# Attention score masks: added by VectorE in the instructions that take the row maxima, instead of by TensorE matmuls

## What is computed

```
def sdpa(q, k, v, bias):                       # 16 heads of 16 features
    s = jnp.einsum('bhqd,bhkd->bhqk', q, k) * scale + bias
    p = jax.nn.softmax(s, axis=-1)
    return jnp.einsum('bhqk,bhkd->bhqd', p, v)

causal_bias = jnp.where(i[None, :] <= i[:, None], 0.0, NEG)       # self, 256 keys
allowed = (j <= seg_ids) & (j > seg_ids - LOOKBACK)               # cross, 4096 keys
cross_bias = jnp.where(allowed, 0.0, NEG)
for l in range(4):
    h = rmsnorm(x, n1[l]);  q, k, v = split(h @ Wqkv[l].T + bqkv[l]);  q, k = rope(q), rope(k)
    x = x + sdpa(q, k, v, causal_bias) @ Wo[l].T + bo[l]
    h2 = rmsnorm(x, n2[l])
    x = x + sdpa(h2 @ Wq_c[l].T, kc, vc, cross_bias) @ Wo_c[l].T  # kc, vc from memory @ Wkv_c[l].T
    h3 = rmsnorm(x, n3[l])
    x = x + silu(h3 @ Wg[l].T) * (h3 @ Wu[l].T) @ Wd[l].T
```

## Time and profile before

| | us |
|---|---|
| median of 3 runs | 621.46 (620.04 to 621.73) |
| span of the profiled execution, first to last instruction | 617.9 |
| TensorE busy | 564.1 (91%) |
| VectorE busy | 353.5 (57%) |
| ScalarE busy | 279.5 (45%) |
| GpSimd busy | 117.7 (19%) |
| mean granted TensorE clock | 0.991 of full |

### The profile page before, as it was taken

One profiled execution on the slowest core, in us unless ns is written; L12 is line 12 of the kernel. 1 busy time (PEld: TensorE's weight loads), 2 busy tenths in 40 slices (PEclk: granted clock), 3 DMA queues, 4 the chain that ended last, 5 costly groups with the idle time before them and its releaser, 6 DMA issues.

```text
span 617.9 us, 13676 instructions
## 1 busy us (share of the span) xinstructions
PE 564.1 (91%) x5806; PEld 421.8 (68%) x5806; DVE 353.5 (57%) x680; ACT 279.5 (45%) x490; POOL 117.7 (19%) x124
## 2 busy tenths in 40 slices
PE   4989998999999899999998989999898989999855
PEld 1666655988767566988766658987666558897523
DVE  5896445466564454674554455574554364752787
ACT  0254444633355336433544446342554547445523
POOL 4252100012323100020612000122312001252110
PEclk9999999999999999999999999999999999999969
DMA  8800020010500200201400200204000200000001
GB/s 334 345 2 25 12 69 2 5 65 1 205 2 4 102 1 3 68 1 27 180 1 36 70 2 2 69 1 189 16 2 1 71 0 2 0 1 2 2 1 39
DMA packets 4676, 30.29 MB, mean 49 GB/s; under 512 B 1153, under 2 KB 1665, under 8 KB 2818
## 3 DMA queue, kind: packets, MB, share of 16 engines
q1 hardware_dynamic: 4610, 29.35, 12.5%
HBM read 28.82 MB, written 0.52 MB: 47 GB/s over the span
## 4 chain that ended last, share of the span: by engine, by line
PE 77%; DVE 10%; ACT 8%; issue 3%; POOL 1%; DMA 1%; SPq 0%; DVEq 0%; POOLq 0%
PE psD L326 18%; PE QD L621 12%; PE psD L634 9%; PE QD L408 6%; PE QD L443 4%; ACT PTR L1253 3%; PE psD L320 3%; PE QD L436 3%; PE QD L394 3%; DVE AQ L1803 3%; PE psD L463 2%; PE QD L431 2%; PE psD L359 2%; PE psD L484 2%; PE psD L470 2%
## 5 line engine op out<-in xcount | busy, mean ns | idle before, releaser
L1253 ACT ACTIVATE PTR<-QD 128x2048 f32<-128x2048 f32 x40 | 75.1, 1878 | 41.8 <-PE QD L443 21.5
L326 PE MATMUL psD<-WAB,hT 128*128 128x256 f32 (+1 forms) x216 | 70.1, 465 | 2.2 <-DVE hT L1744 2.2
L2492 POOL TENSOR_TENSOR rstd<-ms,mhalf 128x2 f32<-128x2 f32 x26 | 19.9, 764 | 271.8 <-DVE ms L1729 270.6
L1803 DVE TENSOR_REDUCE AQ<-QD 128x8 f32<-128x2048 f32 (+1 forms) x24 | 55.0, 2290 | 27.0 <-PE QD L408 27.0
L621 PE MATMUL QD<-HH,WFH 128*128 128x256 f32 x224 | 67.4, 301 | 0.4 <-DVE WFL L1903 0.4
L1903 DVE TENSOR_TENSOR WFL<-WC,WFH 128x512 fp32r<-128x512 f32 x64 | 48.0, 755 | 32.2 <-ACT WFH L1297 32.1
L621 PE MATMUL QD<-HL,WFH 128*128 128x256 f32 x224 | 63.3, 283 | 0.0
L621 PE MATMUL QD<-HH,WFL 128*128 128x256 f32 x224 | 63.3, 283 | 0.0
L1800 DVE TENSOR_REDUCE AQ<-QD 128x16 f32<-128x2048 f32 x16 | 36.7, 2293 | 39.9 <-PE QD L408 39.9
L634 PE MATMUL psD<-WC,HID 128*128 128x256 f32 x256 | 58.2, 380 | 0.0
L326 PEld LDWEIGHTS psD<-WAB,hT 128*128 128x128 f32 x216 | 39.7, 195 | 21.0 <-issue 14.2
(11 more groups left out here) (172 smaller groups left out, 1021.2 us busy)
## 6 DMA issues: line engine op xcount, KB each, us to landing
WC<-in_wc SPq DMA_DIRECT2D x4, 3072.0 KB, 10.9
WAB<-in_wa SPq DMA_DIRECT2D x4, 1024.0 KB, 4.9
WAB<-in_wb SPq DMA_DIRECT2D x4, 1024.0 KB, 4.7
WF<-in_wf SPq DMA_DIRECT2D x1, 3072.0 KB, 22.8
bias<-in_bias SPq DMA_DIRECT2D x4, 512.0 KB, 3.4
WAB<-in_wt SPq DMA_DIRECT2D x1, 1024.0 KB, 6.0
X<-in_x SPq DMA_DIRECT2D x2, 256.0 KB, 2.8
out_x<-X SPq DMA_DIRECT2D x4, 128.0 KB, 2.4
```

The source lines that it names most:

```text
L326: mm = pe.matmul(bank(l, use)[:, col:col + n], lhs(k), rhs(k), start=(k == 0), stop=(k == KT - 1))
L1253: nc.scalar.activation(PTR[:, r % 2, :], QD[:, :], ACT.Exp, scale=SCALE).then_inc(t_exp, 1)
L1803: v = dve.tensor_reduce(QKR[b][:, t, 0, h, MAXROW].rearrange("p (s r) -> p r s", r=SG_H), QD[:, :].rearrange("p (r s n) -> p r s n", r=4, ...
```

## The change

The mask matmuls of `scores` go: the first score matmul of a bank now has `start=True`. `maxima` becomes a run of `tensor_tensor_reduce` instructions, one for each head and tile of queries. Each reads its 128 or 256 scores from PSUM, adds the mask (bf16, SBUF), multiplies by -1, writes the product back to the same place of PSUM, and keeps the running minimum; a second instruction then writes this minimum out. In the lists below the two are `ISA QD,AQ<-QD,causB` and `ISA AQ 128x1`. A round with tiles of 128 keys has 16 of the pairs, a round with 256 keys 8. `causB` grows to 128 x 256, zeros in its first half. The mask matmuls of `scores_T` (L431) stay.

```
@@ scores @@
                 quad_free(s_max, l * ROUNDS + r + 1)
-                for a in range(4):
-                    if cross:
-                        pe.matmul(quad[a].rearrange("p (s n) -> p s n", s=2), identB[:, :],
-                                  maskB[:, 2 * b:2 * b + 2, :].rearrange("p t n -> p (t n)").unsqueeze(1).broadcast_to([P, 2, L]),
-                                  start=True, stop=False, skip_group_check=True)
-                    elif t == 0:
-                        pe.matmul(quad[a].rearrange("p (s n) -> p s n", s=4), identB[:, :],
-                                  causB[:, :].unsqueeze(1).broadcast_to([P, 4, P]), start=True, stop=False, skip_group_check=True)
-                    else:
-                        pe.matmul(quad[a].rearrange("p (s n) -> p s n", s=2)[:, :, P:L], identB[:, :],
-                                  causB[:, :].unsqueeze(1).broadcast_to([P, 2, P]), start=True, stop=False, skip_group_check=True)
...
-                                           QKT[b][rows(a), s, L:L + keys], start=False, stop=True, skip_group_check=True)
+                                           QKT[b][rows(a), s, L:L + keys], start=(at == 0), stop=True, skip_group_check=True)
@@ maxima @@
                 if cross:
-                    v = dve.tensor_reduce(QKR[b][:, :, 0, h, MAXROW].rearrange("p t (s r) -> p r s t", r=SG_H),
-                                          QD[:, :].rearrange("p (r s t n) -> p r s t n", r=4, s=2, t=QT), AX_X, ALU.max, negate=True)
+                    if l == 0:
+                        dve.wait_ge(mask_set, 1)
+                    for a in range(4):
+                        for n, s in enumerate(ss):
+                            for q in range(QT):
+                                v = dve.tensor_tensor_reduce(quad[a][:, (2 * n + q) * P:(2 * n + q + 1) * P],
+                                                             quad[a][:, (2 * n + q) * P:(2 * n + q + 1) * P], maskB[:, 2 * b + q, :],
+                                                             -1.0, NO_MAX, ALU.add, ALU.min,
+                                                             accum_out=QKR[b][:, q, 0, SG_H * s + a, MAXROW:MAXROW + 1])
                 else:
...
+                    keys = (t + 1) * P
+                    for a in range(4):
+                        for n, s in enumerate(ss):
+                            v = dve.tensor_tensor_reduce(quad[a][:, n * keys:(n + 1) * keys], quad[a][:, n * keys:(n + 1) * keys], causB[:, L - keys:L],
+                                                         -1.0, NO_MAX, ALU.add, ALU.min,
+                                                         accum_out=QKR[b][:, t, 0, SG_H * s + a, MAXROW:MAXROW + 1])
@@ DVE, layer @@
                 residual(l, 0, "wo0")
-                cross_kv(l, 0)
+                maxima(l, 5)
                 mean_square(l, 1, 0)
-                maxima(l, 5)
```

More of the change, by code:

```diff
@@ L786, in layer @@
                 pv(l, 5)
+                cross_qT(l, 0, 1)
                 outputs_T(l, 5)
@@ L798, in layer @@
                 cross_kT(l, 1)
+                cross_qT(l, 1, 0)
                 pv(l, 6)
-                cross_qT(l, 1, 0)
+                scores(l, 8)
+                cross_qT(l, 1, 1)
                 outputs_T(l, 6)
-                scores(l, 8)
                 pv(l, 7)
-                cross_qT(l, 1, 1)
                 outputs_T(l, 7)
@@ L932, in _ @@
             cross_qT(0, 0, 0)
+            cross_qT(0, 0, 1)
             outputs_T(0, 4)
-            cross_qT(0, 0, 1)
             scores(0, 6)
             pv(0, 5)
+            outputs_T(0, 5)
             cross_kv(0, 1)
-            outputs_T(0, 5)
             scores(0, 7)
@@ L984, in rest @@
                 out_proj(0, 1, "cwo1", Woc, "coT1")
+                down(0, 0, range(0, 4))
                 gate_up(0, 0, 7)
-                down(0, 0, range(0, 4))
                 norm_T(0, 2, 1)
@@ L1043, in rest @@
                 maxima_T(NL - 1, 4)
-                cross_kT(NL - 1, 0)
                 pv(NL - 1, 3)
                 scores_T(NL - 1, 4)
+                outputs_T(NL - 1, 3)
+                maxima_T(NL - 1, 5)
                 norm_T(NL - 1, 1, 0)
-                maxima_T(NL - 1, 5)
-                outputs_T(NL - 1, 3)
+                cross_kT(NL - 1, 0)
+                scores_T(NL - 1, 5)
                 cross_q(NL - 1, 0)
-                scores_T(NL - 1, 5)
                 pv(NL - 1, 4)
                 cross_qT(NL - 1, 0, 0)
+                scores(NL - 1, 6)
                 cross_qT(NL - 1, 0, 1)
-                scores(NL - 1, 6)
                 outputs_T(NL - 1, 4)
@@ L1111, in rest @@
                 gate_up(NL - 1, 1, 4)
+                down(NL - 1, 1, range(0, 4))
                 gate_up(NL - 1, 1, 5)
@@ L1114, in rest @@
                 gate_up(NL - 1, 1, 7)
-                down(NL - 1, 1, range(0, 4))
                 window_T(0)
@@ L1374, in layer @@
                 self_strips(l, 1, 0, 1)
+                split_high(l, 0)
+                split_high(l, 1)
                 strip_outputs(l, 1)
@@ L2139, in layer @@
                 tokens_low(l, 0)
+                split_low(l, 2)
                 split_low(l, 3)
+                hidden(l, 0, 0)
                 split_low(l, 4)
-                hidden(l, 0, 0)
                 hidden(l, 0, 1)
                 split_low(l, 5)
+                divide(l, 8)
                 hidden(l, 0, 2)
-                divide(l, 8)
+                hidden(l, 0, 3)
                 divide(l, 9)
                 split_low(l, 6)
-                hidden(l, 0, 3)
                 hidden(l, 0, 4)
@@ L2153, in layer @@
                     all_blocks(l, 1)
+                residual(l, 1, "cwo1")
+                split_low(l, 8)
+                mean_square(l, 2, 1)
                 hidden(l, 0, 5)
-                residual(l, 1, "cwo1")
-                mean_square(l, 2, 1)
-                split_low(l, 8)
                 normalise(l, 2, 1)
@@ L2241, in rest @@
             def rest(further):
+                divide(0, 3)
                 weigh_T(0, 1, 0)
-                divide(0, 3)
+                split_low(0, 0)
                 cross_q(0, 0)
+                split_low(0, 1)
+                maxima(0, 6)
                 divide(0, 4)
-                maxima(0, 6)
                 divide(0, 5)
-                cross_kv(0, 1)
                 maxima(0, 7)
                 residual(0, 1, "wo1")
-                split_low(0, 0)
+                cross_kv(0, 1)
                 mean_square(0, 1, 1)
@@ L2255, in rest @@
                 cross_q(0, 1)
-                split_low(0, 1)
+                maxima(0, 8)
                 divide(0, 6)
-                maxima(0, 8)
                 divide(0, 7)
@@ L2378, in rest @@
                 hidden(NL - 1, 0, 0)
+                split_low(NL - 1, 5)
                 hidden(NL - 1, 0, 1)
-                split_low(NL - 1, 5)
-                hidden(NL - 1, 0, 2)
                 divide(NL - 1, 8)
@@ L2384, in rest @@
                 split_low(NL - 1, 6)
+                hidden(NL - 1, 0, 2)
                 hidden(NL - 1, 0, 3)
@@ L2651, in rest @@
                 causal(1, 0)
+                sines(1, 1, 0)
+                sines(1, 1, 1)
+                causal(1, 1)
+                causal(1, 2)
                 add_bo(1, 0)
-                sines(1, 1, 0)
-                causal(1, 1)
-                sines(1, 1, 1)
-                causal(1, 2)
                 causal(1, 3)
```

425 lines of the change are left out of this document (210 added, 215 removed).

## The result

| | before | changed |
|---|---|---|
| median, us | 620.75 (4 runs, 619.56 to 621.73) | 636.35 (4 runs, 634.92 to 638.09) |
| span of the profiled execution, us | 617.9 | 632.8 |
| TensorE / VectorE busy, us | 564.1 / 353.5 | 545.2 / 410.0 |
| mean granted TensorE clock | 0.991 | 0.973 |

The ratio is 1.0252, 95% interval 1.0234 to 1.027: slower.

A forecast was written before the change was run, and what follows sets the result against it. TensorE, busy 564.1 of 617.9 us, was taken as the bound, with maxima narrowly hidden in the QD loop. Adding 24.4 us gave 642.3, and 3.6 around it 646 us; the range was 610 to 682.

The forecast's parts named there:

- A pair of 0.27: VectorE's maxima: main instruction over 128 numbers 0.20 us, accumulator read-out 0.07 us more; 0.40 with 256 numbers.
- Both rivals: VectorE's pairs: read-out hidden, 0.20 to 0.23 us, chance 0.19; or PSUM both ways costs more, 0.30 to 0.34, chance 0.16.
- the slope of the prediction: 520 pairs taken to lie on the path, so each 0.01 us of a pair changes the time by 5.2 us.
- The sum: Whole kernel: +5.0 us a layer, 20 in four, +4.4 in the first layer; 617.9 + 24.4 = 642.3, plus 3.6 around it.
- waits in rounds 0 to 5: TensorE's new waits for longer maxima and lost cover in the first six attention rounds: 6.3 us a layer.
- The estimate of 0.32: Price of a VectorE pair by the skill's overhead figures, in us; it would make the sum some 26 us higher.
- Masks: Four mask matmuls leave each round's scores on TensorE: 7.8 us a layer, 31.3 us in four layers.
- Along the layer: TensorE's new order laid out stretch by stretch with the old lengths: +5.0 us a layer, 20 in four.
- the two signs of being wrong: Pairs under 0.22 us apart, or the waits of rounds 0 to 5 missing.
- the rival of cover in the new order: Rounds 0 to 5: the order hides the forecast waits, 6.3 us a layer, giving 621 us; chance 0.09.
- First layer: Rounds 0 to 3 there: longer maxima of 6.2 us wholly on the path, less 1.8 of waits: +4.4 us.
- The clock: Rival: TensorE's granted clock falls because it has more holes, giving 660 us or more; chance 0.03.

The follow-up runs named there:

- e9: The changed kernel with the product of each pair written to a bf16 tile in SBUF instead of back to PSUM: 613.26 us.
- e12: The old lists of steps with masks added in the pairs and the product in SBUF, f32 for the first bank's pairs in self rounds: 621.71 us.
- e2: The new lists of steps with TensorE's mask matmuls and the one reduction per round of the kernel before: 632.29 us.
- e3: The new lists of steps, no mask matmuls in scores, one reduction per round over unmasked scores: 600.98 us.
- e1: The old lists of steps, with masks added by VectorE in pairs and no mask matmuls in scores: 640.54 us.
- e10: The changed kernel with the old order of steps in the quantised part alone: 634.67 us.
- e6: The changed kernel with useless transposes filling TensorE's waits for the maxima in rounds 3, 5 and 7: 632.54 us.
- e4: The old lists of steps, no mask matmuls in scores, one reduction per round over unmasked scores: 592.49 us.
- e11: Old lists, no mask matmuls in scores, one reduction over unmasked scores, plus useless transposes in two TensorE waits of the quantised part: 593.35 us.
- e5: The changed kernel with one VectorE copy of 128x1 numbers between SBUF tiles ahead of each of the 512 pairs: 648.98 us.

## Why the prediction was right, point by point

**The forecast held; its price was off in two parts that nearly cancel.** A pair of 0.27 was 0.20 + 0.07. Measured is 0.25, which e9 and e12 split into 0.20 + 0.01 + 0.04. I took the read-out for seven times what it costs, by ScalarE's rows, and the write to PSUM for nothing. Both rivals were half true: the read-out is hidden, and the product in PSUM costs more, if only directly behind a read-out. Each alone would have given a pair of 0.21 or of 0.31. That the two nearly cancel is luck. By the slope of the prediction, 0.25 makes 646 - 10.4 = 635.6; 636.35 was measured. Put at 0.21, the same formula gives 646 - 31.2 = 614.8 for e9, which took 613.3. That it comes so close is partly luck too. The sum had nothing for the last stretch (4.5 us longer), for the stretch without rounds (1.1 a layer) and for the clock (3.8), and against that it had waits in rounds 0 to 5 that aren't there.

**Launch and end.** The sum adds 3.6 us for what lies around the span. That was a median less the span of another execution. In one and the same execution it is 1.7 to 1.9 us for the kernel before (beside the experiments), and 2.5 to 3.1 for the changed one, so about 1 us of the loss lies outside the span; what makes it longer isn't shown.

The estimate of 0.32 from the figures of the Trainium skill (Perfetto Trace Analysis, Optimizing Scalar/DVE Operations) is too high by 0.07 here. The second instruction is there in the trace, as the Trainium skill says of accumulator outputs (VectorE: DVE Perf Modes, Two Vector instructions with no wait between them), but lies almost wholly beside its neighbours.

**Masks.** 31.3 us by the sum, 31.3 by e2 and e3, 27.7 in the old lists.

**Along the layer.** +5.0 a layer was forecast, +2.6 by the formula at 0.25; layer 1 shows +2.1, and layer 2, with the longest fall of the clock, +3.4. The cross rounds came out as told once the price is put right: 5.47 and 5.48 us from scores to scores where 5.85 less 16 x 0.02 is 5.53. The stretches of rounds 0 to 3 and 4 to 5 came out at -1.26 and +0.48 where 0 and +1.7 were told; about 0.8 and 0.6 of that is the price, the rest waits that I had laid out and that aren't there. Of the 6.3 us of new waits in rounds 0 to 5 the trace shows some 2.7, the largest 0.62 and 1.40 (before 0.80) at `scores_T` of rounds 3 and 4 and 1.04 (before 0.39) at `cross_q`. That was one of the two signs of being wrong, and it came half true, as did the rival of cover in the new order. The stretch without rounds was forecast at 0 and measured +1.1, which I missed: it is the new order there, since e2 has it too (53.8 us from the maxima of round 9 to those of the next layer, before 52.3, e1 with the old lists 52.6). I called this order harmless because the row of before shows no hole, which says nothing on the holes that a new order makes.

**First layer.** 9.4 us up to layer 1 were forecast, 6.2 at 0.25; the maxima of its round 0 start 6.1 us later (155.64, before 149.50). The number fits, the reason is not shown: e2, with masks and reduction as before, is 5.3 us late there by the new lists alone (154.82), for which the forecast had nothing.

**The last stretch.** From the maxima of round 9 in the last layer to the end of the span it is 123.9 us, before 119.4: 4.5 more, where I had 0, at most 2 either way. 3.0 of them are the quantised part (e10). The failed step is the sentence that steps "change places by one or two", for which I counted nothing.

**The clock** got 0.03. It fell in four places of the attention layers, and e6 prices it at 3.8 us, not the 14 or more of the rival. It lies inside the measured numbers above, so the waits alone are less than they seem. The argument was that windows with 92% busy had kept 1.00; these dips stand behind single holes, which a busy share doesn't show.

**The signs.** TensorE was forecast at 535 us busy and shows 545.2: matmuls at the lower level last longer, as e9 with its clock of 0.989 shows 535.8. VectorE shows 410.0 for 420, and the layer period is 134.9 and 136.2 for 138.

**A version that beats both.** e4 at 592.49, 4.5% below before, if the margin of the unmasked maxima may go. With masked maxima, e9 at 613.26: the change itself with the product written where nobody reads it.

## What to carry to other kernels

Before work moves from a full engine to a half idle one, count what fills and empties the buffer between them: here 28 to 31 us of the time went with the masks, and 35 to 48 came back as waits, because the receiving engine is on the loop of one PSUM buffer. Price an instruction by start-to-start distances, and vary its output as well as its inputs: here it was worth 23 us to write a product that nobody needs to SBUF and not back to PSUM. And test a new order of steps apart from the computation that it comes with; this one gained 4 us around the pairs and lost 12 without them. And look where the clock fell before a median is read as "no gain": in e11 it fell outside the waits that were filled.

## What was not expected of the hardware

- `tensor_tensor_reduce` with its accumulator read-out takes 0.21 us for 128 numbers from PSUM with the product to SBUF, f32 or bf16 alike, and 0.25 with the product to PSUM; 0.345 and 0.38 for 256 (e9, e12, the changed kernel). The read-out's row is 0.08 or 0.14 us long and adds an estimated 0.01 to the 0.20 of a copy from PSUM.
- The 0.04 us between these two are paid only directly behind a read-out: with a copy of 128x1 in between, the main instruction takes 0.21 with its product in PSUM too (e5). So the copy, whose row is 0.15 long and which holds the queue for 0.07, adds only 0.025.
- TensorE's granted clock fell to its lower level around single waits of 0.7 to 1.4 us in the attention layers (the changed kernel at 63.74, 213.46, 370.37 and 470.43 us), and a projection of 1.99 us took up to 3.78. Other waits of 0.9 us left the clock alone.
